# Second attention of a two-layer block: the output product as three fp16 products in place of one fp32 product

## The reference

```python
def _L1_xattn_ref(queries, keys, values, ind_q, ind_k, ind_v, Wq, Wk, Wv, Wo):
    H, HD = (16, 64)
    Q = (queries @ Wq).reshape(b, nq, H, HD).transpose(0, 2, 1, 3) * ind_q[:, None, :, None]
    ...
    scores = jnp.einsum('bhqd,bhkd->bhqk', Q, K) / jnp.sqrt(jnp.float32(HD))
    attn = jax.nn.softmax(scores, axis=-1)
    ...
    out = jnp.einsum('bhqk,bhkd->bhqd', attn, V)
    out = out.transpose(0, 2, 1, 3).reshape(b, nq, H * HD)
    return out @ Wo
...
x = x + _L1_xattn_ref(_layernorm(x, axis=-1), ctx_1024, ctx_1024, mask, mask, mask, Wq, Wk, Wv, Wo)
```

## Time and profile before

| | us |
|---|---|
| median of three runs | 1181.32 |
| lowest and highest | 1177.41, 1184.25 |
| the profiled execution, its own time | 1175.89 |
| its span, first to last instruction | 1174.0 |
| TensorE busy | 907.9 (77%) |
| VectorE busy | 731.3 (62%) |
| ScalarE busy | 579.6 (49%) |
| GpSimd busy | 644.9 (55%) |

### The profile page before, as it was taken

One profiled execution on the slowest core, in us unless ns is written; L12 is line 12 of the kernel. 1 busy time (PEld: TensorE's weight loads), 2 busy tenths in 40 slices (PEclk: granted clock), 3 DMA queues, 4 the chain that ended last, 5 costly groups with the idle time before them and its releaser, 6 DMA issues. The chain is left out here.

```text
span 1174.0 us, 28543 instructions
## 1 busy us (share of the span) xinstructions
PE 907.9 (77%) x10881; PEld 713.1 (61%) x10881; DVE 731.3 (62%) x1778; ACT 579.6 (49%) x954; POOL 644.9 (55%) x656
## 2 busy tenths in 40 slices
PE   2479888765567666299992589898889888898898
PEld 1357676542222222189992488887878887787565
DVE  3567777626577675156551557676867766664787
ACT  1147888756665757056662224343433433433564
POOL 1258898764777775344444644555546354521565
PEclk9998999967777887599996689999999999999999
DMA  6221222009557755777766404042432404001921
GB/s 165 79 75 58 65 79 74 8 9 291 221 192 222 287 212 202 267 200 202 201 184 225 172 22 171 20 169 68 157 95 96 167 20 165 19 3 27 193 70 36
DMA packets 107940, 152.29 MB, mean 130 GB/s; under 512 B 14101, under 2 KB 84674, under 8 KB 101410
## 3 DMA queue, kind: packets, MB, share of 16 engines
q1 hardware_dynamic: 73986, 116.91, 31.0%
q0 software_dynamic: 8480, 20.99, 5.8%
q10 hardware_dynamic: 25344, 12.59, 3.8%
HBM read 84.66 MB, written 65.54 MB: 128 GB/s over the span
## 5 line engine op out<-in xcount | busy, mean ns | idle before, releaser
L1477 POOL DMA_INDIRECT rows_x<-rows_r,index_r x128 | 137.6, 1075 | 68.6 <-issue 36.7
L923 POOL DMA_INDIRECT fetched_a<-rows_y,chosen_row x128 | 126.2, 986 | 82.7 <-DVE att_a L831 49.3
L450 POOL TENSOR_TENSOR p_lo_a<-probs_a,p_hi_a 128x1024 f16<-128x1024 f32 x64 | 136.1, 2132 | 40.2 <-ACT p_hi_a L313 40.0
L646 PE MATMUL psum<-v_x_a,probs_a 128*128 128x65 f32 x1024 | 125.0, 276 | 0.0
L646 PEld LDWEIGHTS psum<-v_x_a,probs_a 128*128 128x128 f32 x1024 | 120.9, 194 | 0.0
L734 ACT ACTIVATE q_a_a<-psum 128x512 f16<-128x512 f32 x64 | 38.2, 597 | 150.3 <-PE psum L666 142.7
L1680 POOL TENSOR_TENSOR h_lo_t<-hidden_t,h_hi_t 96x512 f16<-96x512 f32 x48 | 55.6, 1158 | 86.9 <-ACT h_hi_t L1630 86.9
L816 DVE TENSOR_REDUCE negmax_a<-psum 128x8 f32<-128x1024 f32 x64 | 78.2, 1222 | 30.0 <-remote 21.7
L696 PE MATMUL psum<-wo,att_t_a 128*128 128x128 f32 x512 | 67.3, 287 | 20.7 <-DVE q_b_a L802 18.8
L312 ACT ACTIVATE probs_a<-psum 128x1024 f32<-128x1024 f32 x64 | 65.7, 1027 | 30.0 <-PE psum L170 29.9
L359 DVE TENSOR_REDUCE negmax_a<-psum 128x8 f32<-128x1024 f32 x64 | 77.8, 1215 | 4.1 <-PE psum L186 3.9
(11 more groups left out here) (362 smaller groups left out, 3130.5 us busy)
## 6 DMA issues: line engine op xcount, KB each, us to landing
values<-v_out_r SPq DMA_DIRECT2D x16, 1040.0 KB
v_x_a<-values SPq DMA_DIRECT2D x16, 1040.0 KB, 7.7
keys<-k_out_r SPq DMA_DIRECT2D x16, 1024.0 KB
listed_t<-rows_x SPq DMA_DIRECT2D x96, 128.0 KB, 2.5
rows_y<-result_t ACTq DMA_DIRECT2D x48, 256.0 KB, 2.4
k_a_a<-keys SPq DMA_DIRECT2D x16, 512.0 KB
k_b_a<-keys SPq DMA_DIRECT2D x16, 512.0 KB
share_f<-shares SPq DMA_DIRECT2D x14, 512.0 KB, 8.1
```

The costliest lines, as they stand in the source:

```text
L450: nc.gpsimd.tensor_tensor(p_lo[:, s % RING0, :], probs[:, s % NPR, :], p_hi[:, s % RING0, :], ALU.subtract).then_inc(s_plo, 1)
L646: last_ = nc.tensor.matmul(PV[:, part, i * (HD + 1):(i + 1) * (HD + 1)], probs[:, s % 3, lane(part, i)], v_x[:, par, b % GB, h, :], start= ...
L923: nc.gpsimd.indirect_dma_start(fetched[:, b % NF1, k, :], None, rows_y, bass.IndirectOffsetOnAxis(ap=chosen["row"][:, b, k:k + 1], axis=0) ...
L1477: nc.gpsimd.indirect_dma_start(rows_x, bass.IndirectOffsetOnAxis(ap=index[:, g * GB + t, k:k + 1], axis=0), rows[:, g % 2, t, :, :].rearra ...
```

## The change

The rows of attention and the weight of the output product are each split into two fp16 halves, an upper one and the remainder. The output product becomes three fp16 products per block of 128: upper by upper, upper by lower, lower by upper, 24 fp16 matmuls for 8 fp32 ones. ScalarE's copy of att now writes the upper half as fp16, and VectorE has a new subtraction, once in every slot, from the bank into the lower half; it is this that now sets att's bank free. The halves of the attention rows have two buffers, one for even samples and one for odd. The halves of the weight are made once, ahead of the loop. And out moves from the head of its even slot to the tail, behind nmt and ahead of att.

```diff
     if s % 2 == 0:
-        if 0 <= s - 4 < 2 * B:
-            head.append(("out", (s - 4) // 2))
         if 0 <= s + 4 < 2 * B:
             head.append(("q", ((s + 4) // 2, 1)))
         if 0 <= s + 2 < 2 * B:
             tail.append(("nmt", (s + 2) // 2))
+        if 0 <= s - 4 < 2 * B:
+            tail.append(("out", (s - 4) // 2))
...
-    att, att_t = sb("att", [P, 2, 512]), sb("att_t", [P, 1024])
+    att = sb("att", [P, 2, 512])
+    att_hi, att_lo = sb("att_hi", [P, 2, 1024], F16), sb("att_lo", [P, 2, 1024], F16)
+    wo_hi, wo_lo = sb("wo_hi", [P, 8, D], F16), sb("wo_lo", [P, 8, D], F16)
...
+                    if n == 0:
+                        pe.wait_ge(s_set, 3)
                     for m in range(8):
-                        last_ = nc.tensor.matmul(o[:, 0:D], att_t[:, m * P:(m + 1) * P], w["wo"][:, m, :],
-                                                 start=m == 0, stop=m == 7)
+                        hi, lo = att_hi[:, n % 2, m * P:(m + 1) * P], att_lo[:, n % 2, m * P:(m + 1) * P]
+                        nc.tensor.matmul(o[:, 0:D], hi, wo_hi[:, m, :], start=m == 0, stop=False)
+                        nc.tensor.matmul(o[:, 0:D], hi, wo_lo[:, m, :], start=False, stop=False)
+                        last_ = nc.tensor.matmul(o[:, 0:D], lo, wo_hi[:, m, :], start=False, stop=m == 7)
...
-                    if j == 0 and b:
-                        out_bank, out_n = place[("out", b - 1)]
+                    if j == 0 and b >= 2:
+                        out_bank, out_n = place[("out", b - 2)]
                         act.wait_ge(s_full[out_bank], out_n + 1)
-                    nc.scalar.activation(att_t[:, 512 * j:512 * j + 512], o, ACT.Copy).then_inc(s_free[bank], 1)
+                    nc.scalar.activation(att_hi[:, b % 2, 512 * j:512 * j + 512], o, ACT.Copy).then_inc(s_upper[bank], 1)
...
             act.wait_ge(s_set, 1)
+            nc.scalar.activation(wo_hi[:, :, :], w["wo"][:, :, :], ACT.Copy).then_inc(s_set, 1)
...
+                elif kind == "att":
+                    b, j = divmod(n, 2)
+                    last_ = nc.vector.tensor_tensor(att_lo[:, b % 2, 512 * j:512 * j + 512], o,
+                                                    att_hi[:, b % 2, 512 * j:512 * j + 512], ALU.subtract)
...
+            dve.wait_ge(s_set, 2)
+            nc.vector.tensor_tensor(wo_lo[:, :, :], w["wo"][:, :, :], wo_hi[:, :, :], ALU.subtract).then_inc(s_set, 1)
```

More of the change, by code:

```diff
@@ L788, in shared @@
                 o = SHARED[bank]
-                if kind in ("nmt", "att", "l", "m"):
+                if kind in ("nmt", "l", "m"):
                     return
@@ L796, in shared @@
                     uppers = sum(1 for i, (bk, c) in place.items()
-                                 if bk == bank and c <= count and i[0] in ("x", "q", "y"))
+                                 if bk == bank and c <= count and i[0] in ("x", "q", "y", "att"))
                     dve.wait_ge(s_upper[bank], uppers)
```

## The result

The changed kernel takes 1207.59 us (median of six runs, 1200.22 to 1220.74) against 1180.43 of the kernel before beside it: a ratio of 1.023, 95% interval [1.019, 1.027]. It is slower by 27 us. The forecast was 1183 with a range up to 1199, so the result lies above the range. The trace after is of the slowest of the six executions (1220.74) and that of before of a quick one (1175.89), so the two traces differ by more than the medians do.

The account below looks back on a forecast made before the run. TensorE was taken as nearly full, waiting on VectorE's q subtraction in an ordered chain. The terms +6.3 + 1.7 - 2.2 - 3.9 = +1.9 us, put on the median of 1181.32, gave 1183 us, range 1167 to 1199.

Parts of the forecast that it names:

- The walk: Step-by-step timing of four kinds of slot pair, from Z, the end of q0's subtraction: +1.25 us per eight slots.
- the pair behind a grade: Pair where VectorE's grade delays q1's subtraction, so out waits and x starts later: 1.13 us lost; a bad pair.
- y and l: Pair with y ahead and l in its even slot; x starts at 8.09 instead of 7.56: 0.53 us lost; a bad pair.
- q1 inherits out's wait: At q0's subtraction: the 1.2 us wait stays with another item behind it; nothing gained from out losing it.
- The weight's split: Ahead of the loop: costs nothing, since VectorE and ScalarE are idle; some 2.5 us if that cover were gone.
- the plain pair: Pair without extra items: x starts at 5.88 us and not at 6.41, so 0.53 us is saved.
- the one with m: Pair with m ahead and statistics2 ending its even slot: the 0.53 us saving goes and 0.12 us is lost.
- Ahead of the first y: Five pairs at the stage's start, four at -0.53 us and one with statistics2 at -0.1: -2.2 us.
- The end: After the last q: copy waits go (about 1.9 us), shorter products (2.7), last product waits 0.7 longer: -3.9 us.
- I keep them as they are: Per round, one trickling q0 and VectorE's late maxima: taken as unchanged; all gone -16 us, twice as many +16.
- rival (d): Longer TensorE rests behind grade lower the clock, more q0s trickle: +11 to +23 us, 1194 to 1206; chance 0.20.
- the sum of +1.9: Whole second attention: +6.3 in five rounds, +1.7 more bad pairs, -2.2 early pairs, -3.9 at the end, in us.

Follow-up runs that it names:

- e9: The changed kernel itself again, on a chip where no q0 trickles: 1155.97 us, 1.012 of the kernel before.
- e5: The kernel before, unchanged, run once more on a chip where no q0 trickles: 1139.57 us, ratio 1.000.
- e16: The kernel before with its fp32 output product only moved to the tail of its slot, no halves or subtraction: 1143.80 us, 1.003.
- e6: The changed kernel without VectorE's new subtraction; the upper half is used twice and ScalarE's copy frees the bank: 1131.91 us, 0.994.
- e13: The kernel before with a made rest half way through q0 in one slot a round, six in all: 1164.28 us, 1.019.
- e12: The changed kernel with GpSimd's third gather of every pair made to wait until q0's product is done: 1164.17 us, 1.022.
- e1: The kernel before with only the output product's place moved to the tail, on the first chip group: 1209.13 us, 1.011.
- e14: The changed kernel with a made rest of some 1.8 us in six q0 products, one a round: 1167.45 us, 1.027.
- e17: The changed kernel with even items' halves made by ScalarE (upper, later) and GpSimd (lower), and the grade cut in two: 1166.45 us, 0.987 of the kernel before.
- e18: The changed kernel with both items' halves made by ScalarE and GpSimd, and the grade cut in two: 1192.25 us, 1.010 of the kernel before.
- e3: The changed kernel with 18 unused matmuls in TensorE's wait behind att of every odd slot: 1191.86 us, 1.001 of the kernel before.
- e7: The changed kernel with unused matmuls in four places: behind att in odd and some even slots, ahead of l and behind it: 1149.95 us, 1.010.
- e4: The changed kernel itself once more, on the first chip group, for a second trace: 1215.28 us, 1.019 of the kernel before.
- e15: The changed kernel with VectorE's grade cut in two, without any filler matmuls: 1148.03 us, 1.007 of the kernel before.

## Why the prediction was wrong

**The walk was right in its sum and in the two bad pairs, not in the other two.** At full clock, measured on the chips without trickles (e9 against e5): the pair behind a grade +1.05 (I had +1.13), y and l +0.48 (+0.53), a round +1.37 (+1.25). The bound "q1 inherits out's wait" held: the waits listed under e9 stand at q1, y and m. The weight's split cost nothing that shows. But the plain pair gained 0.02 where I had 0.53, and the one with m gained 0.14 where I had a loss of 0.12; that the sum of the two comes near (-0.16 for -0.41) is luck in part. Ahead of the first y the plain pair is as walked, 11.32 long, with x at Z + 5.90 (5.88). In the steady rounds x waits for GpSimd's normalised rows, for which the walk had no term, and starts at Z + 6.37. Both pairs in e9 (Z at 703.86 and at 776.84):

```profile
709.76 0.33 PE L660 MATMUL psum<-ident,xhat_a 128*128 128x128 f32 x1
...
783.21 0.30 PE L660 MATMUL psum<-ident,xhat_a 128*128 128x128 f32 x1 [0.42 <-POOL xhat_a L930]
```

Ahead of the first y the later pairs gained 2.0, where I had 2.2.

**The end was mis-sized.** From the last q0's subtraction to the next stage before takes 38.58 and the change 36.47: 2.1 gained where I had 3.9. The runs part the three terms: the place gives 2.07 (e16; I had 1.9), the halves without the subtraction 2.03 more (e6; 2.7), and the subtraction takes back 1.99, where I had 0.7.

**The step that failed** is that the sum held no term for the clock. "I keep them as they are" took the trickling q0s and the rests behind them over from before at no further cost, and the fall was left to rival (d), with 0.20. The trickling q0s did stay as they were (their pairs -0.5 in all). What changed is the clock right behind them: in every round of the trace after it falls within 0.7 us of Z, where y starts, and the six y and l pairs take 22.6 us more, of 29.2. Rival (d) had the kind of event right, but three things in it were off:

- The place. It put the long rests in the pair behind a grade. No pair behind a grade has a fall in the trace after.
- The sign of danger. The pair of the earlier trace rows, the one fall that before has in its steady rounds, is a pair behind a grade as well. The y and l pair ahead of it took 15.17, but at clock 1.00; the subtraction of its q0 came late, and the clock fell behind the rest of 2.12 that this made, where the stretch that I had set against (d) has rests of 1.2 (out took 3.42, for 2.05 in the earlier trace rows):

```profile
978.41 3.42 PE L696 MATMUL psum<-wo,att_t_a 128*128 128x128 f32 x16 [2.12 <-DVE q_b_a L802]
```

- The price. I took 1.6 a fall from there, and the falls cost 3.0 to 4.8 on the first chip (16.5 to 18.3 against 13.5), 1.5 on a quiet one.

Against (d) I had only that one stretch with rests of 1.2 stood at 1.00, and it is of a pair without a trickle. How small the reserve is, e13 shows: in the kernel before, on a chip without trickles, one made rest of 1.66 in q0 is enough for a fall. The range ended at the middle of (d). That the upper end of (d), 1206, lies near the result is luck, since its place was wrong and its price too small.

On the quiet chips the sum of +1.9 can be held against a stage that is 12.9 longer in e9 than in e5. Of that the four falls are 6.2. The remaining 6.7 is some 5 over the forecast: 2.5 at the first pairs of the stage, which vary from run to run (the third one takes 9.95 in e5, 12.16 in e9 and 10.14 in e12), 0.2 in the later pairs ahead of the first y, 0.6 in the rounds and 1.7 at the end. There too the change is slower.

**What stays open.** It is open why the clock falls behind the trickling q0 in the change and not before: the rests listed there are nearly the same (1.33 ahead of y before, 1.37 after), and e1 falls there too, without halves or subtraction. The rests go ahead of the falls and fillers in their place hold the clock, but not every round with the same rests falls, and the depth differs between chips; e14 didn't reproduce the first chip's depth by adding the trickle's rest. What makes q0 trickle was not isolated: it stands beside four gathers in a row, but on the quiet chips the same four do no harm, and e12, meant to part them, landed on such a chip. In e17 and e18, with a subtraction between the third and fourth gather, the trickle is 1.1 us instead of 2.1, which fits the gathers as its cause; but the kernel before was not traced on that chip.

## What to carry to other kernels

Before you move an engine's wait, list TensorE's rests in each kind of pair, not on average, and give the clock a term of its own in the sum. The pair that has lost the clock once needn't be the one that loses it after the change; the places to watch here were the rest behind the slowest q0 and the pair with the most rests, and a fall there cost 1.5 to 4.8 us. Splitting the fp32 operand into fp16 halves saved 1.5 us a round here, and the subtraction cost 2.1, since VectorE is a link of the ring: cost such a step in the order in which its engine works, and look for a slot in which another one waits. Try such a change with matmuls in the rests (e3, e7): what comes back was the clock's, and what stays is the waits'.

## What the hardware showed that I had not expected

- **Chips differ by 40 to 50 us for one kernel.** The kernel before: 1180 to 1190 on three, 1140 on three others. On two of those at 1180 to 1190 one q0 a round takes 2.1 us from its first matmul to its last, with rests marked "issue", while GpSimd issues four gathers in a row; on those at 1140 the same four gathers are there and q0 takes 0.62 (pairs of 13.9 against 11.84). The stage also begins 8 to 31 us later on those at 1180 to 1190.
- **Matmuls without use were free here and held the clock where they stood.** 18 in a wait of about 1 us cost the kernel before nothing (1.001) and made the stage of the changed one 12.4 us shorter; with more of them in the other rests (e7) no fall was left.
- **The clock falls in two places.** Behind a trickling or made rest in q0 it falls around the start of y (after, e1, e4, e13, e14), without one, or with the rest ahead of y filled (e3), some 10 us later, behind the rests ahead of l and x (e3, e9, e15).
- **A wait on GpSimd is passed on.** One that should only space gathers (e12) made x wait 2.33 us, 9 us later.
